# Two gated attention and mixture-of-experts layers on one core: one store of the second layer's output rows, the attentions' first loads a stage ahead, other counts of filling transposes

## The chip, the cores and the metric

The kernel runs on 1 core of one Trainium2 chip. The metric is the device time of one execution in microseconds (us), lower is better. Before the change it is 845.72 us (median of 3 runs, 845.16 to 845.79). A difference of about 0.2% (1.7 us) is what a measurement of this kernel can tell from no change.

## The reference, cut to what matters

Two layers, each a gated cross-attention and then a gated mixture of experts, over x of 8 batches x 256 tokens x 256 features (2048 tokens), all in float32:

```python
x = x + tanh(g_xattn[0]) * attention0(layernorm(x), ctx)        # 16 heads of 16, keys and values from ctx
x = x + tanh(g_ffn[0])   * moe0(layernorm(x))                   # 8 experts, top 2, gelu, biases
x = x + tanh(g_xattn[1]) * attention1(layernorm(x), ctx)
x = x + tanh(g_ffn[1])   * moe1(layernorm(x))                   # 7 experts and a no-op one, top 2, capacity 256

# moe1: weights = softmax(router logits); keep the top 2; each expert takes its first 256 tokens
combined = zeros.at[used_idx].add(relu(inputs @ inter) @ out * in_w)
combined = combined + x_flat * (noop_w * noop_mask)             # the no-op expert's rows
```

So the second layer's result for each token is a sum of three things: x after the attention, its normalised row times its no-op weight, and up to two rows from experts.

## The kernel before, in words

The program is five stages one after the other, each closed by a barrier of all engines that also clears its semaphores (line 77): a small one for constants, then for each layer an attention stage and a stage of routing and experts. Within a stage each engine (SP issues plain DMAs; POOL, ACT, DVE and PE compute; POOL also issues indirect DMAs) runs a list written out by hand, in order, with semaphore waits. An instruction that waits holds up all behind it on its engine.

**Constants** (`constants_phase`): SP loads the gates; POOL makes the identity matrix and index tables; DVE makes the head masks; ACT takes the tanh.

**Attention** (`attention_phase`), by batches b = 0 to 7 of 256 tokens. At its start SP issues, in this order: x of batch 0, Wq, bq, ctx 0, Wk, bk, x of batch 1, Wv, bv, ctx 1, x 2, bo, Wo, and the rest. DVE takes moments of batch 0, POOL turns them into a scale (`rows_scale`, L299 and L301), DVE normalises (L579), PE transposes (`x_transpose(0)`), ACT writes the high part of the transposed rows (L427) and DVE the low part (`inputs_low`, L651), and PE makes `queries(0)`. Each matrix is kept as a high and a low part: ACT writes the high one (`weight_high`, L462) and waits for the weight's load and its bias's by one semaphore; DVE writes the low one (`weight_low`, L647). ctx is split by POOL (`split_context`, L335 and L337). Where PE would stand still, transposes of the identity keep it busy (`fill_first`, `fill_last`, L98); their counts are written in PE's list. In layer 0 DVE first makes nine small tables for the routing (`route_constants`, L551 to L561). At the end of each batch SP stores the normalised rows xr to `xw` (L269) and x to `x1` in layer 0, to `out` in layer 1 (L271), 256 KB each.

**Routing** (`route_phase`): a chain of small DVE instructions over the logits gives the list of tokens per block of 256 slots (`token_of`). Its tables lie in the memory of the x tile and in a tile `more`. In layer 1 ACT meanwhile multiplies xr by the no-op weights (L1258, 16 instructions).

**Experts** (`expert_phase`), by blocks: 23 in layer 0 (16 of 256 slots, 7 of 128), 7 in layer 1. Per block, two sets of 1 MB of weights are loaded (in layer 0 by POOL's indirect DMA at L1161, in layer 1 by SP at L1538 and L1541), split into high and low parts by ACT (L1616, L1624) and DVE (L1688, L1699), the block's rows are gathered by POOL (`load_x`, L1556), transposed by PE (`turn`, L1786), split by ACT (L1656) and DVE (`inputs_low`, L1757), and multiplied. PE's order is first product of block b, in which the rows of block b+1 are turned after the third of four parts, and then the second product of block b-1. Between the products ACT evacuates (L1632 or L1635) and DVE splits the hidden values (`hidden_parts`, L1711 and L1713). DVE's order in a block puts `inputs_low(b + 1)` behind three of the four `hidden_parts`. POOL adds the weighted results to DRAM rows by indirect accumulating DMAs (`add_to_tokens`, L1581).

In layer 1, POOL's list runs: rows of blocks 0, 1 and 2; then four DMAs that add the scaled xr to `out` in DRAM (L1596, 512 KB each, `accum_op`); then for each block b the rows of block b+3 and the additions of block b. The first additions wait for those four DMAs. SP's list in layer 1's experts runs: weights of block 1's first half done, then `load_weights(b)` for b = 0, 1, ...: first set of block b+2, second set of block b+1, each behind the split that frees its buffer.

Of the kernel before, what the change touches and what calls it, by code (L numbers as in the profile page):

```python
# [9 lines left out]
ALU = mybir.AluOpType  # L10
# [90 lines left out]
def attention_phase(nc, layer, shared, dram):  # L101
# [4 lines left out]
    with ExitStack() as ctx:  # L106
# [15 lines left out]
        w_raw = {n: sb(f"{n}_raw", [P, KC, D]) for n in ("wq", "wk", "wv", "wo")}  # L122
# [89 lines left out]
        def _(sp):  # L212
            ctx_src = dram["ctx_t"].rearrange("(k p) n -> p k n", p=P)
            w3 = {n: dram[n].rearrange("(k p) n -> p k n", p=P) for n in ("wq", "wk", "wv", "wo")}
# [19 lines left out]
            def load_weight(n, done):  # L234
                sp.dma_start(w_raw[n][:, :, :], w3[n]).then_inc(done, 16)
# [12 lines left out]
            sp.dma_start(bo[:, :], dram["bo"]).then_inc(wo_ld, 16)  # L248
            load_weight("wo", wo_ld)
# [14 lines left out]
            x_dst = dram["out" if layer else "x1"][0:N, :].rearrange("(t p) d -> p t d", p=P)  # L264
# [27 lines left out]
            sp.wait_ge(x_stored, 16 * B)  # L292

        @block.gpsimd
        def _(pool):
# [34 lines left out]
            def split_context(b):  # L330
                pool.wait_ge(ctx_ld[b % CB], 16 * (b // CB + 1))
# [3 lines left out]
                pool.tensor_copy(hi[:, :, :], ctx_raw[b % CB][:, :, :]).then_inc(ctx_hi, 1)  # L335
                pool.wait_ge(ctx_hi, b + 1)
                pool.tensor_tensor(lo[:, :, :], ctx_raw[b % CB][:, :, :], hi[:, :, :].bitcast(F32), ALU.subtract).then_inc(ctx_split, 1)  # L337
# [56 lines left out]
        def _(act):  # L394
# [12 lines left out]
            def queries(b):  # L407
                wait(act, st_ps, CH * (b - 2))
                if b == 0:
                    act.wait_ge(wq_ld, 32)  # L410
                project(b, q_ps, q_evac, bq, q_s[b % 3][0])

            def keys(b):
                if b == 0:
                    act.wait_ge(wk_ld, 32)
# [42 lines left out]
            loads = {"wq": wq_ld, "wk": wk_ld, "wv": wv_ld, "wo": wo_ld}  # L458

            def weight_high(n):  # L460
                act.wait_ge(loads[n], 32)
                act.activation(w[n][0][:, :, :], w_raw[n][:, :, :], ACT.Copy).then_inc(w_hi[n], 1)  # L462

            def scale_bias():
                act.wait_ge(wo_ld, 32)
# [83 lines left out]
        def _(dve):  # L549
# [14 lines left out]
            def moments(b):  # L564
                if b < XP:
# [16 lines left out]
            def values(b):  # L582
                if b == 0:
                    dve.wait_ge(value_ones_set, 1)
                    dve.wait_ge(wv_ld, 32)
# [74 lines left out]
            if layer == 0:  # L660
                route_constants()
# [7 lines left out]
            moments(2)  # L669
            values(0)  # L670
# [91 lines left out]
        def _(pe):  # L762
# [150 lines left out]
            fill_first(24)  # L913
            x_transpose(0)
            fill_first(12)
            queries(0)
            fill_first(8)
            keys(0)
            fill_first(8)
            values(0)  # L920
            head_scores(0, 0)
            fill_first(4)
            x_transpose(1)
            head_scores(0, 1)
            fill_first(5)
            head_scores(0, 2)
            fill_first(6)
            queries(1)
            head_scores(0, 3)
            fill_first(4)  # L930
            head_scores(0, 4)
            keys(1)
            head_scores(0, 5)
            fill_first(4)
            head_scores(0, 6)
            values(1)
            head_scores(0, 7)
            fill_first(3)
            x_transpose(2)
            fill_first(4)  # L940
            max_transpose(0)
            fill_first(4)
            head_scores(1, 0)
            queries(2)
            head_scores(1, 1)
            scores(0, 0)
            head_scores(1, 2)
            keys(2)
            head_scores(1, 3)
            weigh_values(0, 0)  # L950
# [1001 lines left out]
```

## Time and profile before

| | us |
|---|---|
| median of 3 runs | 845.72 (845.16 to 845.79) |
| profiled execution, its own time | 845.71 |
| its span (first to last instruction) | 844.0 |
| PE busy | 752.9 (89%) |
| DVE busy | 603.9 (72%) |
| ACT busy | 478.4 (57%) |
| POOL busy | 382.4 (45%) |
| DMA moved | 103.45 MB |

The page shows, for each engine, its busy time; then busy tenths in 40 slices of 21.1 us; then DMA queues, the chain of work that ended last, and the costliest groups of instructions. In the slices PE's digit is 9 nearly everywhere; it falls at the start of each layer (slices 1 and 24), in the routing of each layer (slices 11 and 12, 34 and 35), at slice 37 (from 760 us) inside layer 1's experts, and at the end. The stages, by the first instructions behind each barrier: attention 0 from 4.6 us, routing and experts 0 from 214.1, attention 1 from 502.5, routing and experts 1 from 711.7. Lines are those of the kernel before.

### The profile page before, as it was taken

Reading aid. Unit: us, or ns where it says so; the run is one execution under the profiler, and the core shown is the slowest. Engines: PE = TensorE matmul, PEld = TensorE weight load, DVE = VectorE, ACT = ScalarE, POOL = GpSimd, SP = SyncE. Lnnn points to the kernel's source line nnn. Section 1 sums busy time; section 2 is a strip of 40 time slices with the busy share of each in tenths; the row PEclk is TensorE's granted clock in tenths of the full one; section 3 lists DMA queues with packets and bytes.
Section 4 is the critical chain, followed back from the end, with each engine's and each line's share of the span. In section 5 each row is a group of like instructions: output and inputs, shape, how many; then the busy total and the mean of one; then the engine's idle time right before and its main releaser. Section 6 shows DMA issues by size and latency. Waiting matters only on the chain. (4 is left out here: it accounts for less than half of the span.)

```text
span 844.0 us, 17413 instructions
## 1 busy us (share of the span) xinstructions
PE 752.9 (89%) x6872; PEld 636.0 (75%) x6872; DVE 603.9 (72%) x1212; ACT 478.4 (57%) x722; POOL 382.4 (45%) x379
## 2 busy tenths in 40 slices
PE   6999999999469999999999948999999998295995
PEld 5666667667369999999999946666677667295995
DVE  4777777753769998998998916777777734774882
ACT  3376666753056777777676603676667661553640
POOL 6465444112145766666666326645551130252532
PEclk9999999999779999999999979999999999587998
DMA  7001000010377888888888336001000013398642
GB/s 231 15 21 40 27 27 23 9 50 32 98 276 218 243 259 251 256 251 253 254 254 253 74 58 192 14 15 40 27 28 27 28 43 117 97 304 220 165 86 28
DMA packets 47697, 103.45 MB, mean 123 GB/s; under 512 B 9952, under 2 KB 38240, under 8 KB 39936
## 3 DMA queue, kind: packets, MB, share of 16 engines
q0 software_dynamic: 18912, 67.56, 28.0%
q1 hardware_dynamic: 28704, 34.78, 12.3%
q8 instruction: 55, 0.90, 0.4%
q14 instruction: 26, 0.21, 0.1%
HBM read 84.22 MB, written 17.83 MB: 121 GB/s over the span
## 5 line engine op out<-in xcount | busy, mean ns | idle before, releaser
L598 DVE TENSOR_REDUCE mx_a<-ps_max_a 128x2 f32<-128x512 f32 x256 | 164.2, 685 | 35.5 <-PE ps_max_a L844 35.2
L89 PE MATMUL ps_h_e<-xe_t_e,w_e 128*128 128x256 f32 (+1 forms) x480 | 137.9, 287 | 6.0 <-DVE xe_t_e L1757 6.0
L450 ACT ACTIVATE prob_a<-ps_st_a 128x2048 f32<-128x2048 f32 x64 | 120.1, 1876 | 29.1 <-PE ps_st_a L863 28.7
L90 PE MATMUL ps_h_e<-xe_t_e,w_e 128*128 128x256 f32 (+1 forms) x480 | 134.9, 281 | 0.0
L91 PE MATMUL ps_h_e<-xe_t_e,w_e 128*128 128x256 f32 (+1 forms) x480 | 134.9, 281 | 0.0
L89 PE MATMUL ps_y_e<-w_e,h_e 128*128 128x256 f32 x424 | 118.5, 279 | 0.0
L90 PE MATMUL ps_y_e<-w_e,h_e 128*128 128x256 f32 x424 | 118.0, 278 | 0.0
L91 PE MATMUL ps_y_e<-w_e,h_e 128*128 128x256 f32 x424 | 117.9, 278 | 0.0
L89 PEld LDWEIGHTS ps_h_e<-xe_t_e,w_e 128*128 128x128 f32 x480 | 93.0, 194 | 8.2 <-DVE xe_t_e L1757 8.2
L91 PEld LDWEIGHTS ps_h_e<-xe_t_e,w_e 128*128 128x128 f32 x480 | 92.7, 193 | 0.0
L90 PEld LDWEIGHTS ps_h_e<-xe_t_e,w_e 128*128 128x128 f32 x480 | 92.7, 193 | 0.0
L844 PE MATMUL ps_max_a<-k_r_a,q_r_a 32*128 32x512 f32 x256 | 82.8, 513 | 4.0 <-DVE mx_a L598 1.1
L318 POOL TENSOR_SCALAR r_var_eps_a<-r_mean_var_a 128x2 f32<-128x2 f32 x16 | 3.6, 228 | 180.0 <-DVE r_mean_var_a L625 180.0
L1161 POOL DMA_INDIRECT w_raw_w<-L_w,block_row x46 | 48.5, 1055 | 80.6 <-DVE b_e L1704 55.4
L1581 POOL DMA_INDIRECT x<-y_e,token_of x39 | 68.6, 1760 | 30.7 <-ACT y_e L1647 17.4
L1556 POOL DMA_INDIRECT xe_e<-normalised_weighted,token_of x53 | 61.7, 1163 | 45.4 <-DVE token_of L1467 28.0
L89 PEld LDWEIGHTS ps_y_e<-w_e,h_e 128*128 128x128 f32 x424 | 79.9, 188 | 0.0
L91 PEld LDWEIGHTS ps_y_e<-w_e,h_e 128*128 128x128 f32 x424 | 79.9, 188 | 0.0
L90 PEld LDWEIGHTS ps_y_e<-w_e,h_e 128*128 128x128 f32 x424 | 79.8, 188 | 0.0
L1713 DVE TENSOR_TENSOR h_e<-hid_e,h_e 128x512 fp32r<-128x512 f32 (+1 forms) x120 | 76.1, 634 | 4.1
L863 PE MATMUL ps_st_a<-q_s_a,k_s_a 32*128 32x256 f32 x1024 | 78.0, 395 | 0.3
L1635 ACT ACTIVATE hid_e<-ps_h_e,b_e 128x256 f32<-128x256 f32 (+1 forms) x184 | 71.0, 445 | 8.1 <-PE ps_h_e L91 7.6
(236 smaller groups left out, 1756.0 us busy)
## 6 DMA issues: line engine op xcount, KB each, us to landing
w_raw_w<-L_w SPq DMA_DIRECT2D x14, 1024.0 KB
ctx_raw_a<-ctx_t SPq DMA_DIRECT2D x16, 256.0 KB, 4.2
normalised_weighted<-xr SPq DMA_DIRECT2D x16, 256.0 KB, 2.2
x_sb<-x SPq DMA_DIRECT2D x8, 256.0 KB
x_sb<-x SPq DMA_DIRECT2D x2, 1024.0 KB, 8.6
x<-x_sb SPq DMA_DIRECT2D x8, 256.0 KB, 2.5
out<-x_sb SPq DMA_DIRECT2D x8, 256.0 KB, 2.5
out<-xr POOLq DMA_DIRECT2D x4, 512.0 KB, 21.9
```

The lines of the kernel that those rows point to most:

```text
L89: pe.matmul(out, lhs[0], rhs[0], start=start, stop=False)
L90: pe.matmul(out, lhs[1], rhs[0], start=False, stop=False)
L91: return pe.matmul(out, lhs[0], rhs[1], start=False, stop=stop)
L450: act.activation(prob[n % 2][:, :, :, :], ps_st[:, :, :, :], ACT.Exp, scale=HD ** -0.5).then_inc(prob_ready, 1)
L598: dve.tensor_reduce(mx[:, q, h:h + HG + 1:HG], ps_max[j][:, :, :], AX.X, ALU.max).then_inc(max_done, 1)
L844: pe.matmul(ps_max[j][:, :, :], q_r[b % 2][r:r + 32, c, q * P:(q + 1) * P], k_r[b % 2][r:r + 32, c, :, :], start=True, stop=True).then_inc ...
L863: ins = pe.matmul(ps_st[:, g, kt, :], k_s[b % 3][c % 2][rows, c // 2, kt * P:(kt + 1) * P], q_s[b % 3][c % 2][rows, c // 2, :], start=True ...
L1161: pool.indirect_dma_start(out=buffers[which + "_raw"][b % 2][:, :], out_offset=None, in_=dram[which], in_offset=bass.IndirectOffsetOnAxis( ...
L1556: pool.indirect_dma_start(out=xe[b % 2][:, q, :], out_offset=None, in_=dram["xw"], in_offset=bass.IndirectOffsetOnAxis(ap=shared["token_of ...
L1581: pool.indirect_dma_start(out=dram["out" if layer else "x1"], out_offset=bass.IndirectOffsetOnAxis(ap=shared["token_of"][:, t:t + 1], axis=0),
L1635: ins = act.activation(hid[jp % 2][:, j, 0:w], ps_h[jp % RB][:, j, 0:w], ACT.Gelu, bias=b1[b % 2][:, 2 * jp + j:2 * jp + j + 1])
L1713: dve.tensor_tensor(h[b % 2][1][:, js, 0:w], hid[jp % 2][:, :, 0:w], h[b % 2][0][:, js, 0:w].bitcast(F32), ALU.subtract).then_inc(h_ready, 1)
```

## The change

Three things, all in one edit.

1. **Layer 1's output.** The attention of layer 1 no longer stores x to `out`. The routing's tables move out of the x tile, into the memory of `more`, `hid`, `y`, `xe` and the second `w2_raw`, so that x stays in its tile. POOL adds the scaled xr to x there, in four `tensor_tensor` instructions of 128x1024, two before the gather of block 2's rows and two behind it; SP stores each quarter once to `out` with a plain DMA, in its list behind `load_weights(0)` and before `load_weights(1)`. POOL's first additions wait for these stores.
2. **First loads.** Wq, Wk, Wv, Wo and ctx 0 and 1 get places in the upper three quarters of the xr tile and semaphores of their own. For layer 0 SP issues x of batch 0, Wq, Wk, ctx 0, Wv and ctx 1 in the constants stage, for layer 1 all six (without x) in the experts stage of layer 0, once four of its blocks are weighed. `route_constants` of layer 0 moves behind `moments(2)` in DVE's list.
3. **Fills.** PE's list is written out once per layer, with other counts of filling transposes at its head: before `x_transpose(0)`, `queries(0)`, `keys(0)` and `x_transpose(1)` they were 24, 12, 8 and 4; they are 12, 6, 4 and 3 in layer 0, and 23, 6, 4 and 3 in layer 1. All other entries are as before.

The diff, cut to its core:

```diff
@@ attention_phase, SP @@
-            load_x(0)
-            load_weight("wq", wq_ld)
+            if layer:
+                load_x(0)
             sp.dma_start(bq[:, :], dram["bq"]).then_inc(wq_ld, 16)
-            load_context(0)
-            load_weight("wk", wk_ld)
             sp.dma_start(bk[:, :], dram["bk"]).then_inc(wk_ld, 16)
             load_x(1)
-            load_weight("wv", wv_ld)
             sp.dma_start(bv[:, :], dram["bv"]).then_inc(wv_ld, 16)
-            load_context(1)
             load_x(2)
             sp.dma_start(bo[:, :], dram["bo"]).then_inc(wo_ld, 16)
-            load_weight("wo", wo_ld)
+            if layer == 0:
+                load_early(sp, 0, shared, dram, ("wo",))
...
                 sp.dma_start(xr_dst[:, tiles, :], xr[:, tiles, :]).then_inc(xr_stored, 16)
-                sp.wait_ge(x_done, b + 1)
-                sp.dma_start(x_dst[:, tiles, :], x[:, tiles, :]).then_inc(x_stored, 16)
+                if layer == 0:
+                    sp.wait_ge(x_done, b + 1)
+                    sp.dma_start(x_dst[:, tiles, :], x[:, tiles, :]).then_inc(x_stored, 16)
@@ ACT: the weights wait for their own loads, the biases' users for the biases @@
             def weight_high(n):
-                act.wait_ge(loads[n], 32)
+                act.wait_ge(first_ld[n], 16)
@@ DVE @@
-            if layer == 0:
-                route_constants()
             moments(0)
...
             moments(2)
+            if layer == 0:
+                route_constants()
@@ PE, layer 0 (layer 1: 23, 6, 4, ..., 3) @@
-            fill_first(24)
+                fill_first(12)
                 x_transpose(0)
-            fill_first(12)
+                fill_first(6)
                 queries(0)
-            fill_first(8)
+                fill_first(4)
                 keys(0)
...
-            fill_first(4)
+                fill_first(3)
                 x_transpose(1)
@@ new @@
+def load_early(sp, layer, shared, dram, names):
+    for n in names:
+        if n[:3] == "ctx":
+            out = shared["first_ctx"][int(n[3:])]
+            src = dram["ctx_t"].rearrange("(k p) n -> p k n", p=P)[:, :, int(n[3:]) * S:(int(n[3:]) + 1) * S]
+        else:
+            out, src = shared["w_raw"][n], dram[f"L{layer}_{n}"].rearrange("(k p) n -> p k n", p=P)
+        sp.dma_start(out[:, :, :], src).then_inc(shared["first_ld"][layer][n], 16)
@@ constants_phase, SP @@
             sp.dma_start(gates[:, :], dram["gates"]).then_inc(g_ld, 16)
+            src = dram["x"].rearrange("(t p) d -> p t d", p=P)
+            sp.dma_start(shared["x"][:, 0:QT, :], src[:, 0:QT, :]).then_inc(shared["first_ld"][0]["x"], 16)
+            load_early(sp, 0, shared, dram, ("wq", "wk", "ctx0", "wv", "ctx1"))
@@ expert_phase, SP @@
+            out_dst = dram["out"][0:N, :].rearrange("(t p) d -> p t d", p=P)
             for b in range(blocks):
                 load_weights(b)
+                if b == 0:
+                    for c in range(TT // CT):
+                        sp.wait_ge(out_summed, c + 1)
+                        tiles = slice(c * CT, c * CT + CT)
+                        sp.dma_start(out_dst[:, tiles, :], shared["x"][:, tiles, :]).then_inc(buffers["out_stored"], 16)
+        if layer == 0:
+            sp.wait_ge(y_ready, 4)
+            load_early(sp, 1, shared, dram, ("wq", "wk", "ctx0", "wv", "ctx1", "wo"))
@@ expert_phase, POOL @@
             elif layer:
-                pool.wait_ge(buffers["out_added"], 16 * (TT // CT))
+                pool.wait_ge(buffers["out_stored"], 16 * (TT // CT))
...
         load_x(1)
         if layer:
-            load_x(2)
-            out_dst = dram["out"][0:N, :].rearrange("(t p) d -> p t d", p=P)
-            for c in range(TT // CT):
+            def add_rows(c):
                 tiles = slice(c * CT, c * CT + CT)
                 pool.wait_ge(buffers["noop_scaled"], c * CT + CT)
-                pool.dma_start(out_dst[:, tiles, :], shared["xr"][:, tiles, :],
-                               accum_op=ALU.add).then_inc(buffers["out_added"], 16)
+                pool.tensor_tensor(shared["x"][:, tiles, :], shared["x"][:, tiles, :], shared["xr"][:, tiles, :],
+                                   ALU.add).then_inc(out_summed, 1)
+            add_rows(0)
+            add_rows(1)
+            load_x(2)
+            add_rows(2)
+            add_rows(3)
             for b in range(blocks):
                 load_x(b + 3)
                 add_to_tokens(b)
```

## Rows read from the trace of the kernel before

**Rows 1.** Chain of waits, experts of layer 1: start us, length us, what.
```profile
748.25 24.28 DMA xe_e<-normalised_weighted,token_of
772.57 1.13 PE ps_x_e L1786 x4
...
786.48 0.48 PE ps_x_e L1786 x4
...
798.03 0.48 PE ps_x_e L1786 x4
```
**Rows 2.** Windows: length, busy of each engine (instructions), PEclk, DMA share, GB/s.
```profile
762.40:772.60 10.20, 0.03 (x1) 0.03 (x1) 4.62 (x7) 0.75 (x2) 0.00 (x0) 0.72 0.90 284
774.00:776.00 2.00, 2.00 (x11) 2.00 (x11) 1.45 (x3) 1.28 (x2) 1.70 (x2) 0.50 0.58 60
```
**Rows 3.** Timeline, POOL: start, us, line, operation, [idle before it and its releaser].
```profile
735.45 0.94 POOL L1556 DMA_INDIRECT xe_e<-normalised_weighted,token_of  x1 [0.30 <-issue]
...
772.72 1.62 POOL L1581 DMA_INDIRECT out<-y_e,token_of  x1 [22.66 <-DMA out<-xr]
```
**Rows 4.** The page, DMA issues: count, KB each, us to landing.
```profile
out<-xr POOLq DMA_DIRECT2D x4, 512.0 KB, 21.9
```
**Rows 5.** By tile xe_e, from 690 us: landing of the gathers.
```profile
DMA to landing us min/median/max: 2.8/4.7/6.8
```
**Rows 6.** Groups by form, POOL: busy us, mean ns.
```profile
L314 POOL TENSOR_TENSOR x_sb<-x_sb,tgbo_a 128x512 f32<-128x512 f32 x16 | 20.4, 1283 | 0.7
```
**Rows 7.** Timelines of POOL and DVE at the start of layer 1.
```profile
508.53 1.80 POOL L337 TENSOR_TENSOR ctx_t_lo_a<-ctx_raw_a,ctx_t_hi_a 128x512 fp32r<-128x512 f32 x1
...
508.52 0.68 DVE L647 TENSOR_TENSOR wq_lo_a<-wq_raw_a,wq_hi_a 128x512 fp32r<-128x512 f32 x1
509.31 1.57 DVE L647 TENSOR_TENSOR wk_lo_a<-wk_raw_a,wk_hi_a 128x512 fp32r<-128x512 f32 x1
```
**Rows 8.** Timelines of DVE and PE, experts of layer 1, blocks 0 to 2.
```profile
737.55 0.17 DVE L1751 COPY slot_weight_e<-xe_e 128x2 f32<-128x2 f32 x1 [3.33 <-ACT xe_t_e L1656]
...
744.68 0.43 DVE L1711 CAST h_e<-hid_e 128x512 fp32r<-128x512 f32 x1 [0.59 <-ACT hid_e L1632]
...
756.82 0.69 DVE L1757 TENSOR_TENSOR xe_t_e<-ps_x_e,xe_t_e 128x512 fp32r<-128x512 f32 x1
...
757.96 0.28 PE L89 MATMUL ps_h_e<-xe_t_e,w_e 128*128 128x256 f32 x1
```
**Rows 9.** Timeline, SP: the issue of block 3's first weights.
```profile
739.14 0.43 SPq L1538 DMA_DIRECT2D w_raw_w<-L_w  x1
```
**Rows 10.** Timelines of SP, DVE and PE at the start of the program.
```profile
0.80 0.39 SPq L1090 DMA_DIRECT2D gates_sb<-gates  x1
...
3.47 0.21 DVE L1105 TENSOR_SCALAR one_row<-in_pair_f 128x1 f32<-128x1 f32 x2
...
4.66 5.00 PE L98 MATMUL ps_st_a<-ident 128*128 128x128 f32 x24 [4.66 <-PEq L77]
5.06 0.46 SPq L235 DMA_DIRECT2D wq_raw_a<-L_wq  x1
...
7.44 0.75 DVE L570 BATCH_NORM_STATS2 stats_a<-x_sb 128x6 f32<-128x256 f32 x2 [0.69 <-DMA x_sb<-x]
...
14.21 0.36 PE L89 MATMUL ps_lin_a<-xn_t_hi_a,wq_hi_a 128*128 128x256 f32 x1 [1.70 <-DVE xn_t_lo_a L651]
```
**Rows 11.** Timelines of DVE and PE at the start of layer 1.
```profile
505.27 0.75 DVE L570 BATCH_NORM_STATS2 stats_a<-x_sb 128x6 f32<-128x256 f32 x2 [13.65 <-DMA x_sb<-x]
...
511.63 0.36 PE L89 MATMUL ps_lin_a<-xn_t_hi_a,wq_hi_a 128*128 128x256 f32 x1 [1.01 <-DVE xn_t_lo_a L651]
```
**Rows 12.** Waits of SP: us in total, times, longest.
```profile
SPq L292 <- DMA out<-x_sb: 2.0, 1, 2.0
```
**Rows 13.** Timelines of POOL and ACT, experts of layer 0: a weight set's issue and first use.
```profile
295.28 0.97 POOL L1161 DMA_INDIRECT w_raw_w<-L_w,block_row  x1 [0.81 <-DVE b_e L1704]
...
310.44 1.07 ACT L1624 ACTIVATE w_e<-w_raw_w 128x1024 fp32r<-128x1024 f32 x1
```

More of the change, by code:

```diff
@@ L120, in halves @@
             return [sb(f"{name}_{part}", shape, F32R) for part in ("hi", "lo")]
-        w_raw = {n: sb(f"{n}_raw", [P, KC, D]) for n in ("wq", "wk", "wv", "wo")}
+        w_raw, first_ctx, first_ld = shared["w_raw"], shared["first_ctx"], shared["first_ld"][layer]
         w = {n: halves(n, [P, KC, D]) for n in ("wq", "wk", "wv", "wo")}
@@ L262, in _ @@
             xr_dst = dram["xw"][0:N, 0:D].rearrange("(t p) d -> p t d", p=P)
-            x_dst = dram["out" if layer else "x1"][0:N, :].rearrange("(t p) d -> p t d", p=P)
+            x_dst = dram["x1"][0:N, :].rearrange("(t p) d -> p t d", p=P)
             def store_router_rows(b):
@@ L564, in moments @@
             def moments(b):
-                if b < XP:
+                if b == 0 and layer == 0:
+                    dve.wait_ge(first_ld["x"], 16)
+                elif b < XP:
                     dve.wait_ge(x_ld[b], 16)
@@ L930, in _ @@
[L930 to L947, printed above, removed]
@@ L993, in _ @@
-            head_scores(B - 2, 0)
-            weigh_values(B - 4, 2)
-            head_scores(B - 2, 1)
-            queries(B - 1)
-            scores(B - 3, 0)
-            head_scores(B - 2, 2)
-            router_turn(3)
-            weigh_values(B - 4, 3)
-            router_logits(3)
-            head_scores(B - 2, 3)
-            turn_heads(B - 4, 1)
-            keys(B - 1)
-            head_scores(B - 2, 4)
-            scores(B - 3, 1)
-            head_scores(B - 2, 5)
-            values(B - 1)
@@ L1169, in route_phase, with sb @@
     tg = shared["tanh_g"][:, 2 + layer:3 + layer]
-    spare = [shared["x"][:, :, :].rearrange("p a b -> p (a b)"), tiles["more"][:, :]]
-    room = [TT * D, MORE]
-    taken = [0, 0]
-    def sb(name, shape, dt=F32, home=0):
+    spare = [tiles["more"][:, :]] + [tile[:, :, :].rearrange("p a b -> p (a b)") for tile in tiles["later"]]
+    spare.append(buffers["w2_raw"][1][:, 0:FC * D])
+    room = [MORE] + [math.prod(tile.shape[1:]) for tile in tiles["later"]] + [FC * D]
+    taken = [0] * len(spare)
+    def sb(name, shape, dt=F32):
         n = math.prod(shape[1:])
         words = n if dt in (F32, I32) else n // 2
+        home = [i for i in range(len(spare)) if taken[i] + words <= room[i]][0]
         at = taken[home]
         taken[home] += words
-        assert taken[home] <= room[home], name
         ap = spare[home][:, at:at + words]
@@ L1526, in expert_phase @@
     listed, comb_stored = sem("listed"), sem("comb_stored")
-    tiles = {"more": sb("more", [P, MORE]), "ps_h": ps_h, "ps_y": ps_y, "listed": listed, "comb_stored": comb_stored}
+    tiles = {"more": sb("more", [P, MORE]), "later": hid + y + xe, "ps_h": ps_h, "ps_y": ps_y, "listed": listed, "comb_stored": comb_stored}
     def sync_part(sp):
@@ L1869, in sb @@
             return ctx.enter_context(nc.sbuf_tensor(name, shape, dt))
+        sem = semaphores(nc, ctx)
         shared = {
@@ L1898, in program @@
         }
+        shared["w_raw"] = {n: shared["xr"][:, TT // 2 + KC * i:TT // 2 + KC * (i + 1), :] for i, n in enumerate(("wq", "wk", "wv", "wo"))}
+        shared["first_ctx"] = [shared["xr"][:, TT // 4 + KC * i:TT // 4 + KC * (i + 1), :] for i in range(2)]
+        first = ("wq", "wk", "ctx0", "wv", "ctx1", "wo")
+        shared["first_ld"] = [{n: sem(f"{n}_first{layer}") for n in first} for layer in range(2)]
+        shared["first_ld"][0]["x"] = sem("x_first0")
         constants_phase(nc, shared, dram)
```

478 lines of the change are left out of this document (338 added, 140 removed).

## The prediction, made before the changed kernel ran

> **What bounds the kernel now.** The page first: PE is busy 752.9 us, 89% of the span (the table above), so a change that leaves PE's work alone can win only where PE stands still or runs at its lower clock. The slices of the page say where that is: the start of each layer, the routings, and one hole inside layer 1's experts. The chain of waits then names the hole. From 748.25 us it runs for 24.28 us through the landing of one gather of rows, and from 772.57 through PE's turn of them [rows 1]. Later turns are 11.55 us apart (798.03 - 786.48), the length of a block that waits for nothing; the turn at 786.48 comes 13.91 us behind the late one [rows 1]. The windows show PE idle from 762.4 to 772.6 with the 16 DMA engines 90% busy, and then at a granted clock of 0.50, the 1.2 GHz level [rows 2].
>
> That late gather is block 3's. On POOL's queue it stands behind the four accumulating DMAs to `out`, which landed a median of 21.9 us after their issue [rows 4]; other gathers took 2.8 to 6.8 us, 4.7 in the median [rows 5]. The first additions of expert results waited 22.66 us for the same four DMAs [rows 3], but nothing of PE's hangs on those.
>
> **The hole in layer 1's experts: 12.8 us to win.** PE began block 2 at 757.96 [rows 8] and turns block 3's rows after 36 of a block's 96 matmuls, 4.2 to 4.3 us on at 11.55 / 96 each: due at 762.2, it came at 772.57: 10.4 us. The following block took 13.91 - 11.55 = 2.4 us more, at the lower clock for its first part. Sum 12.8 us. In the new kernel block 3's gather is issued behind four POOL additions and no accumulating DMA. POOL is free from 735.45 + 0.94 = 736.4 [rows 3]. One addition of 128x512 takes 1.283 us [rows 6], one of 128x1024 is estimated at 2.5. Two of them end at 741.5, the gather of block 2 at about 744 (needed 11.55 us before 762.2, at 750.6; with 4.7 us of landing it comes at 748, with 6.8 at the very edge), the other two at 749 to 750, and block 3's gather is issued by 752 and there by 757 to 759, for 762.2. So the wait goes, unless a queue is fuller than I think. ACT's scaling of xr, which the additions wait for, is over by then.
>
> **What takes its place: POOL against DVE, 4.1 us back.** At the start of layer 1, POOL's L337 was begun at 508.53 and took 1.80 us, not its usual 1.27, while DVE's `wq_lo` ran to 509.20; then DVE's `wk_lo`, begun at 509.31, took 1.57 us instead of 0.68, and ended 0.55 us behind POOL's instruction [rows 7]. Read together, the two engines took turns, each waiting for the whole of the other's. These DVE instructions have two inputs in SBUF. Now the additions 3 and 4 fall at 744 to 749, where DVE has its densest work of just that kind (hidden values, weight parts). If they shut each other out, DVE loses 2 x 2.5 = 5.0 us, less its pause of 0.59 at 744.68 [rows 8]: 4.4. Its slack is small: the low part of block 2's rows was ready at 756.82 + 0.69 = 757.51, and PE began block 2 at 757.96 [rows 8], 0.4 us of slack, since that instruction stands behind six of the hidden ones and four weight parts. So PE waits 4.4 - 0.4 = 4.0, and about 0.1 for a copy of slot weights that the first addition may hold; 4.1. Bounds: 0, if the pair is not exclusive or DVE always goes first, and 5.5 (4.4 - 0.4, and 1.5 if the copy ahead of `inputs_low(0)`, at 737.55 [rows 8], waits for the end of the first addition at 738.95). I take 4.1, from the row that shows the taking of turns. Later blocks catch up: DVE has 10.3 us of work in 11.55. Net 12.8 - 4.1 = 8.7.
>
> The Trainium skill has a rule that speaks against this change here: "GPSIMD Engine Reference", section "Specifications", says that GpSimd's SBUF interfaces are shared with VectorE, in contention where a DVE instruction has two SBUF inputs or a 2-port mode. The trace agrees [rows 7]. By the page the DMA issue moved to arithmetic costs DVE something; without it the net would read 12.8.
>
> **SP's list in that stage.** Behind `load_weights(0)` SP now waits for the four additions, issues four stores (0.33 to 0.47 us each) and only then block 3's first weights, which were issued at 739.14 [rows 9] and will be at about 751. Also behind: block 2's second set (before 749.20, now 751.5). They are first used at 755.2 and 761.5. At 5.9 us from issue to use for such a set when it was waited for (ACT's first weights of layer 0), the first comes at 757: ACT splits it 2 us later than before, which its own pauses cover. I cost this at nothing; without cover it is 2 us. The four plain stores are issued between 739 and 751 and are there by 756; POOL's first additions need them at 760.5. The 2 MB go out once instead of twice (stored, then read and rewritten), so the engines are emptier.
>
> **The attention of layer 1** gives up eight stores on SP, which is idle there; only the last counts: SP's last wait was 2.0 us for it [rows 12], issued 0.4 us behind the store of xr, which now is the last. 0.2 us, between 0 and 0.5.
>
> **Start of layer 0: 2.2 us.** SP now issues six more loads before the first barrier: each takes up to 0.46 us and some 0.05 to the next [rows 10], so from 1.2 it ends at 4.2, where DVE ended at 3.7 [rows 10] and PE began 0.97 later. The barrier moves to 5.15. But x of batch 0 has landed, and DVE's nine tables are out of the way: moments begin at 5.2 instead of 7.44. From there the queries began 6.77 us on (14.21 - 7.44) in layer 0 [rows 10] and 6.36 us on (511.63 - 505.27) in layer 1 [rows 11], where the weights came no later than needed. 5.2 + 6.36 = 11.56, for 14.21: 2.65 us. From the queries to the first head scores both layers took 7.1 us, and the rest of the attention 191 us in both, so the shift carries through. Against it: PE's fills fell from 24 to 12, so there is a pause of about 1 us before the first transposes; the 24 ran at 0.208 us each (5.00 / 24) [rows 10]. If the higher level comes later, 12 matmuls of queries and as many of keys cost 0.1 us each more. I take 0.45 off: 2.2. Bounds: 4 (moments that no other load delays, weights split early, no taking of turns) and 0 (both products at 1.2 GHz, 2.4 us). The moved tables, about 2 us, fit DVE's idle 5 us before `values(0)`.
>
> **Start of layer 1: 0.4 us.** x of batch 0 still can be loaded only behind the barrier. The 6.36 us stay, because the piece that sets them is `wk_lo` behind POOL's L337 [rows 7], and ctx 0 landing earlier only lets POOL begin 0.2 us sooner, into the same taking of turns. The x load shares the engines with fewer others: 0.4, between -0.4 (POOL gets in between DVE's two `xn` instructions) and 1.2.
>
> **Loads of 1.5 MB in layer 0's experts**, at about 297 us: a second weight set there was issued at 295.28 and first used at 310.44 [rows 13], 15 us for a landing of 5 to 6. Nothing; without cover 3 to 5.
>
> **The sum** against the profiled execution's own 845.71: 8.7 + 0.2 + 2.2 + 0.4 = 11.5, so 834.2. The median of the runs is 845.72, the same.
>
> **The rivals.**
> - *No taking of turns.* All 12.8 come back: 845.7 - 15.6 = 830.1. For it: before, POOL was at its DMA issues in the same stretch and DVE hardly slower. Against it: rows 7. 25%.
> - *The starts give nothing:* the barrier is later and the clock is lower, and in layer 1 POOL gets in first. 845.7 - 8.9 = 836.8. 12%.
> - *Block 3's rows stay late,* as two stores and three weight sets share the engines with their gather: at 15 us of landing instead of 4.7 they come at 767, so that 5 us of waiting and the 2.4 us of lower clock stay, and DVE's loss hides in them: 12.8 - 7.4 = 5.4 won, with 2.8 elsewhere 837.5. For it: 24.28 us in rows 1; against it: the accumulating DMAs are what filled the queue. 7%.
> - *Slower: SP is held by the additions.* If DVE goes first at each turn, additions 3 and 4 finish late, and SP, which waits for them, issues no weights for blocks 2 to 4. With the fourth addition ending at T, block 3's first set is issued at T + 0.4, there 5.9 later and split 4.6 later (its halves at 2 us on ACT, then DVE), needed at 769.8. PE waits T + 10.9 - 769.8, plus 2.4 for the clock. That exceeds all that is won (15.6) from T = 772, 9 us an addition instead of 2.5. Then 846 and more, 848 at T = 774. DVE's pauses before that make it unlikely: 3%.
> - *The change does not do what it says:* the early loads or stores cost what they save somewhere, 844 to 847: 3%.
>
> **How the numbers follow.** The forecast has 50%, its own range 832 to 836.5. The range 829 to 839 takes in the rivals down to 830.1 and up to 837.5, and the bounds of the unknown costs. Faster by over 0.2% (1.7 us, about what a measurement of this kernel can tell from no change): 0.94. Within: 0.02. Slower: 0.04.
>
> **What would show each step.** No DMA_DIRECT2D on POOL; a turn of block 3 with no wait for its gather; four POOL TENSOR_TENSOR of 128x1024 at about 2.5 us each; DVE instructions of hidden and weight parts beside the last two at well over 0.69 and 1.22 us; PE waiting some 4 us in all for `inputs_low` or hidden parts in blocks 1 and 2. Moments at 5.2 and queries at 11.6 in layer 0; moments to queries still near 6.4 in layer 1. It would be wrong if DVE's instructions keep their length beside POOL's (then 830), if PE still waits for a gather, or if PE waits for `w_raw_w` through SP's order.

## The result: 843.26 us, a fifth of what was forecast

| | median of the runs, us | from to (runs) | profiled execution, own time | its span |
|---|---|---|---|---|
| before | 845.51 | 844.7 to 848.66 (20) | 845.71 | 844.0 |
| changed | 843.26 | 839.73 to 846.31 (20) | 844.3 | 842.6 |

The ratio is 0.9969, 95% interval 0.9957 to 0.9982: faster by 0.3%, 2.3 us, where 11.5 were forecast. The changed kernel's runs spread over 6.6 us, those of before over 4.

**Where the time went.** Three marks cut the two spans; all are instructions of the two traces.

| us | before | changed | won | forecast |
|---|---|---|---|---|
| start to layer 0's first head scores | 21.32 | 22.73 | -1.41 | 2.2 |
| first head scores to layer 1's first moments | 483.95 | 483.94 | 0.0 | 0 |
| layer 1: first moments to first head scores | 13.47 | 17.53 | -4.06 | 0.4 |
| first head scores to last router logits | 189.96 | 189.81 | 0.15 | 0 |
| last logits to the end (attention's tail, routing, experts) | 135.3 | 128.59 | 6.7 | 8.9 |

The sum is 1.4, the difference of the spans. Against the forecast 3.6 us are missing in layer 0's start, 4.5 in layer 1's and 2.2 in the last part.

**The hole is gone.** The waits of PE behind 715 us in the changed kernel (what PE waited for: us in total, times, longest):

```profile
PE ps_x_e L1979 <- DMA xe_e<-normalised_weighted,token_of: 6.7, 1, 6.7
PE ps_h_e L1457 <- DVE w_raw_w L1632: 6.5, 2, 5.9
PE ps_h_e L89 <- DVE xe_t_e L1950: 6.2, 3, 4.8
```

Only the first rows of the stage are still waited for; the late gather of [rows 1] is gone, and the turns of blocks 3 to 5 are 11.55 us apart. The second row is the routing, whose tables now lie in the memory of the second `w2_raw`; before, PE waited 6.0 us there too. The third row has grown: PE waits for DVE's low part of the rows, 6.2 us in all, where before it waited 1.5 us once. The chain of waits says why (start us, length us, what):

```profile
740.90 1.15 PE ps_x_e L1979 x4
742.05 0.02 issue
742.07 0.61 ACT xe_t_e L1849
742.68 0.02 issue
742.70 3.52 DVE slot_weight_e L1944
746.23 0.60 DVE xe_t_e L1950
```

A copy of 128x2 elements that took 0.17 us [rows 8] takes 3.52. POOL's timeline of the same stretch, then DVE's:

```profile
740.58 0.95 POOL L1745 DMA_INDIRECT xe_e<-normalised_weighted,token_of  x1 [0.30 <-issue]
741.55 4.64 POOL L1783 TENSOR_TENSOR x_sb<-x_sb,xr 128x1024 f32<-128x1024 f32 x2
747.09 0.97 POOL L1745 DMA_INDIRECT xe_e<-normalised_weighted,token_of  x1 [0.90 <-DVE xe_t_e L1950]
748.37 0.94 POOL L1745 DMA_INDIRECT xe_e<-normalised_weighted,token_of  x1 [0.30 <-issue]
749.33 4.72 POOL L1783 TENSOR_TENSOR x_sb<-x_sb,xr 128x1024 f32<-128x1024 f32 x2
```
```profile
742.70 3.52 DVE L1944 COPY slot_weight_e<-xe_e 128x2 f32<-128x2 f32 x1 [3.40 <-ACT xe_t_e L1849]
746.14 0.68 DVE L1950 TENSOR_TENSOR xe_t_e<-ps_x_e,xe_t_e 128x512 fp32r<-128x512 f32 x1
750.47 3.88 DVE L1904 CAST h_e<-hid_e 128x512 fp32r<-128x512 f32 x1 [3.65 <-ACT hid_e L1825]
754.39 0.69 DVE L1906 TENSOR_TENSOR h_e<-hid_e,h_e 128x512 fp32r<-128x512 f32 x1
```

The additions take 2.3 to 2.4 us each, near the 2.5 forecast. But DVE's copy ends at 746.22, behind both additions (746.19), and its cast at 754.35, behind both of the second pair (754.05). DVE did not get in between two additions: it waited for the whole pair. Nor does a wait in POOL's list let it in as such: each addition has one ahead of it, for ACT's scaling, but it was long met, and the second addition began without a gap.

**The same at both starts.** Layer 0, timelines of DVE, POOL and PE:

```profile
5.11 0.75 DVE L570 BATCH_NORM_STATS2 stats_a<-x_sb 128x6 f32<-128x256 f32 x2 [1.42 <-PEq L77]
7.42 3.54 DVE L579 TENSOR_SCALAR xn_a<-x_sb,mean_var_a,rstd_a 128x256 f32<-128x256 f32 x2 [1.27 <-POOL rstd_a L296]
```
```profile
7.47 0.61 POOL L335 CAST ctx_t_hi_a<-xr 128x512 fp32r<-128x512 f32 x1
8.16 1.26 POOL L337 TENSOR_TENSOR ctx_t_lo_a<-xr,ctx_t_hi_a 128x512 fp32r<-128x512 f32 x1
9.36 1.45 POOL L352 MEMSET v_a<- 128x512 f32 x3
10.76 0.66 POOL L335 CAST ctx_t_hi_a<-xr 128x512 fp32r<-128x512 f32 x1
```
```profile
11.01 1.12 PE L766 MATMUL ps_lin_a<-ident,xn_a 128*128 128x128 f32 x4 [3.11 <-DVE xn_a L579]
11.92 1.49 PE L98 MATMUL ps_st_a<-ident 128*128 128x128 f32 x6
14.40 0.55 PE L89 MATMUL ps_lin_a<-xn_t_hi_a,wq_hi_a 128*128 128x256 f32 x1 [1.00 <-DVE xn_t_lo_a L651]
14.75 0.41 PE L90 MATMUL ps_lin_a<-xn_t_hi_a,wq_lo_a 128*128 128x256 f32 x1
```

Moments begin at 5.11, as forecast. The two xn instructions together took 0.73 us in layer 0 before, 0.41 each with some overlap. Here POOL's L335 began 0.05 us behind the start of the first, which took 0.81 and ended 0.14 behind L335, in the gap of 0.08 us that POOL leaves before L337. The second took 2.81: it ended 0.14 behind the last of the three memsets, so it was kept out through L337 and all of them. The next L335 did not hold it, although it began without a gap (10.76, while the last memset lasted to 10.81). Why DVE got in there is not explained; what stood before it is a memset, which reads nothing. PE, its fills done, stood still for 3.11 us and came back at 0.22 us a matmul (14.75 to 14.97), where run e7 below has 0.12 to 0.13. Layer 1 shows the same: moments at 506.67, xn 3.42 us, an idle 3.29 us of PE, queries at 515.85, 9.18 us behind the moments instead of 6.36 [rows 11], and a window inside them at a granted clock of 0.50, the 1.2 GHz level, with the same 0.21 to 0.22 us a matmul (the column of layer 0's start reads 1.00 all through, so there the pitch has to tell):

```profile
517.00:519.00 2.00, 2.00 (x12) 2.00 (x11) 1.13 (x6) 0.15 (x1) 0.00 (x0) 0.50 0.02 7
```

### The profile page after: what moved, and what is told of

Its sections match the earlier page's. It is cut to its first block and busy times, and to the rows that moved or that the text cites. A ratio compares the mean times of both kernels' runs of the same rounds, so it can differ in the third digit from the quotient of the medians.

```text
span 842.6 us, 17351 instructions
## 1 busy us (share of the span) xinstructions
PE 752.0 (89%) x6837; PEld 634.0 (75%) x6837; DVE 616.1 (73%) x1212; ACT 477.6 (57%) x722; POOL 385.9 (46%) x379
## 5 line engine op out<-in xcount | busy, mean ns | idle before, releaser
L1881 DVE TENSOR_TENSOR w_e<-w_raw_w,w_e 128x1024 fp32r<-128x1024 f32 x60 | 72.6, 1218 | 1.2 <-ACT w_e L1809 1.2
```

Of the source, the lines that this page charges most:

```text
L1881: ins = dve.tensor_tensor(w1[b % 2][1][:, k, :, :], w1_raw[b % 2][:, k * F:(k + 1) * F].rearrange("p (j f) -> p j f", j=FC), w1[b % 2][0][ ...
```

## The experiments

Theory HOLD: a DVE instruction that needs what POOL's run holds waits until POOL pauses for a semaphore, however many instructions the run has. Rival TURNS, the forecast's: the two alternate instruction by instruction. In all of them "before" ran on the same chip; the ratio and its interval are against it. Times are medians of the runs; xn is the length of the pair in layers 0 and 1, the marks are those above (first head scores of layer 0, last logits of layer 0, moments to first scores in layer 1, last logits to the end).

| | us (from to, runs) | ratio, 95% | xn | scores 0 | logits 0 | start 1 | last part |
|---|---|---|---|---|---|---|---|
| before | 845.5 | | 0.73, 1.03 | 21.32 | 211.12 | 13.47 | 135.3 |
| changed | 843.26 (839.73 to 846.31, 20) | 0.9969, 0.9957 to 0.9982 | 3.54, 3.42 | 22.73 | 212.55 | 17.53 | 128.6 |
| e1_store_once | 838.33 (837.85 to 839.57, 4) | 0.9902, 0.9882 to 0.9923 | 0.74, 0.74 | 21.46 | 211.25 | 13.59 | 127.7 |
| e2_early_only | 850.36 (846.8 to 852.52, 12) | 1.0042, 1.0027 to 1.0057 | 3.44, 3.41 | 22.81 | 212.61 | 17.73 | 135.5 |
| e3_gap | 841.94 (838.98 to 845.38, 9) | 0.9948, 0.9927 to 0.9969 | 1.03, 3.41 | 18.59 | 208.57 | 18.04 | 128.3 |
| e4_dve_adds | 838.96 (835.54 to 845.46, 6) | 0.9916, 0.9883 to 0.9949 | 3.41, 3.44 | 23.45 | 213.24 | 17.89 | 123.4 |
| e5_start_gap | 839.39 (838.44 to 841.5, 6) | 0.992, 0.9907 to 0.9934 | 2.14, 2.06 | 20.29 | 210.16 | 15.38 | 129.3 |
| e6_start_wait | 839.13 (838.66 to 839.36, 6) | 0.9918, 0.9905 to 0.9931 | 0.74, 0.73 | 17.92 | 210.62 | 12.36 | 128.4 |
| e7_fills | 842.81 (841.73 to 843.99, 6) | 0.9963, 0.9949 to 0.9978 | 3.56, 3.41 | 21.55 | 211.74 | 16.85 | 128.3 |
| e8_both | 831.84 (831.2 to 833.99, 5) | 0.9834, 0.9818 to 0.9849 | 0.73, 0.74 | 17.43 | 211.45 | 12.34 | 123.1 |
| e9_both_fills | 832.15 (831.85 to 832.58, 5) | 0.984, 0.9823 to 0.9857 | 0.73, 0.73 | 19.41 | 209.44 | 12.34 | 122.7 |
| e10_once_dve | 833.85 (833.26 to 834.57, 4) | 0.9862, 0.9841 to 0.9882 | 0.73, 0.73 | 21.04 | 210.82 | 13.84 | 122.2 |
| e11_ones_first | 830.94 (830.16 to 831.54, 5) | 0.9825, 0.9808 to 0.9842 | 0.73, 0.73 | 18.74 | 208.72 | 12.27 | 122.8 |
| e12_late_ctx | 842.75 (839.86 to 851.08, 12) | 0.9975, 0.9955 to 0.9995 | 0.73, 3.41 | 17.47 | 211.14 | 17.58 | 128.2 |

**The two halves of the change.** e1_store_once is the kernel before with part 1 alone; e2_early_only is the changed kernel with part 1 taken back, so parts 2 and 3 alone.

> The kernel before with part 1 alone (x summed by POOL, stored once); starts of both attentions as before. In the changed kernel's trace the attention of layer 1 ends 5.3 us later than before, and the experts stage is 6.5 us shorter. Theory HOLD (a DVE instruction that needs the shared access waits through a whole run of POOL instructions that has no semaphore wait inside; the starts lose by that, and the additions cost DVE 3.4 + 3.5 us): about 845.5 - 6.7 = 838.8, DVE's slot-weight copy and its first cast of hidden values 3 to 4 us long each. Rival TURNS (the engines take turns instruction by instruction, and the rest of the loss is DMA or clock): copy and cast not over 2.6 us, time 836 to 838. If the two parts hinder each other (xr used by both): clearly above 840.

> The changed kernel with part 1 undone (x stored by the attention, xr added by POOL's accumulating DMAs): parts 2 and 3 alone. HOLD: both starts lose, 1.4 us in layer 0 and 4.0 us in layer 1, in the profile each by DVE's second normalising instruction held for about 2.8 us behind POOL's split, memsets and next split, and by queries at the 1.2 GHz level: about 850 to 851. Rival: the starts gain as I predicted and the changed kernel lost its time elsewhere: 842 to 843.

Both came as HOLD expected. Part 1 alone is 1.0% faster than before, parts 2 and 3 alone are 0.4% slower. In e2 both xn pairs are held (3.44, 3.41). In e1 both POOL pairs hold DVE, 3.62 and 3.90 us, with ordinary starts, so the two losses are separate.

**Additions with a pause.** e3_gap makes POOL wait for its own last addition:

```diff
                 pool.wait_ge(buffers["noop_scaled"], c * CT + CT)
+                wait(pool, out_summed, c)
                 pool.tensor_tensor(
```

> The changed kernel with one wait more: each of POOL's additions waits for the semaphore of the one before it, which puts a pause of some 0.08 us between them. HOLD: DVE's slot-weight copy gets in behind the first addition (about 1.3 us instead of 3.5), the first cast behind the third (about 2.3 instead of 3.9): 2 us or so less, 841. TURNS, or a hold by anything but POOL's run of instructions: no change, 843.3.

DVE's timeline in e3:

```profile
739.80 1.27 DVE L1945 COPY slot_weight_e<-xe_e 128x2 f32<-128x2 f32 x1 [3.35 <-ACT xe_t_e L1850]
740.98 0.68 DVE L1951 TENSOR_TENSOR xe_t_e<-ps_x_e,xe_t_e 128x512 fp32r<-128x512 f32 x1
745.31 3.33 DVE L1905 CAST h_e<-hid_e 128x512 fp32r<-128x512 f32 x1 [3.65 <-ACT hid_e L1826]
748.68 2.74 DVE L1907 TENSOR_TENSOR h_e<-hid_e,h_e 128x512 fp32r<-128x512 f32 x1
```
```profile
738.69 4.86 POOL L1784 TENSOR_TENSOR x_sb<-x_sb,xr 128x1024 f32<-128x1024 f32 x2
...
745.91 4.95 POOL L1784 TENSOR_TENSOR x_sb<-x_sb,xr 128x1024 f32<-128x1024 f32 x2
```

The copy now ends at 741.07, in the pause behind the first addition, and the cast at 748.64, between the third and the fourth; the next instruction is then held through the fourth. Both pauses are 0.15 us long. So the pause is what lets DVE in: this is what TURNS had assumed for every pair of instructions. The cast took 3.33 us, not the 2.3 expected. It was begun 0.60 us ahead of the third addition and did not go through before it; POOL was at the issue of a gather then (744.96 to 745.91), with the addition 0.01 us behind it, so the issue may count as part of the run, but no run tests that. The pauses let DVE in but gave no time back here: the last part is 128.3 us against 128.6, and what the median gained (841.94 against 843.26) lies within the spread of both and goes with a start of layer 0 that was not held (below).

**Additions on DVE.** e4_dve_adds (changed kernel) and e10_once_dve (the e1 kernel) put the four additions into DVE's list:

```diff
-                pool.tensor_tensor(shared["x"][:, tiles, :], ...
+            dve.tensor_tensor(shared["x"][:, tiles, :], ...
...
+                if layer:
+                    add_rows(0)
+                    add_rows(1)
                 inputs_low(0)
+                if layer:
+                    add_rows(2)
+                    add_rows(3)
```

> The changed kernel with the four additions on DVE instead of POOL, two before and two behind the low part of block 0's rows, where DVE stands still; SP's stores as they are. HOLD and TURNS alike say that without additions on POOL no DVE instruction is stretched in blocks 0 to 2: four times 1.22 us on DVE in its pauses, the experts stage shorter by about 6 us than the changed kernel's: 837 to 838. If the loss in this stage is SP's order or the DMA queues instead: 841 to 843.

> The kernel before with part 1 alone (output stored once), its four additions on DVE. HOLD: the 4.3 that DVE and PE lost come back, 838.3 - 4.3 = 834.0; no DVE instruction of blocks 0 and 1 is stretched. If POOL's additions cost nothing themselves (the loss was at the starts): 838.

DVE does each in 1.22 us, about half of POOL's 2.36:

```profile
734.89 2.35 DVE L1765 TENSOR_TENSOR x_sb<-x_sb,xr 128x1024 f32<-128x1024 f32 x2
738.34 0.17 DVE L1753 COPY slot_weight_e<-xe_e 128x2 f32<-128x2 f32 x1 [1.09 <-ACT xe_t_e L1658]
...
742.75 0.43 DVE L1713 CAST h_e<-hid_e 128x512 fp32r<-128x512 f32 x1 [1.39 <-ACT hid_e L1634]
```

This is e10. No instruction is stretched, and the last part falls by 5.2 us (changed to e4) and 5.5 (e1 to e10): the price of the hold, forecast at 4.1. The medians fall by 4.3 (changed to e4, whose six runs lie 9.9 us apart) and 4.5. Against before, e10's last part is 13.1 us shorter: that is the hole, forecast at 12.8 and 0.2 for the tail.

**A pause, or a wait, at the starts.** e5_start_gap puts a pause of POOL ahead of the memsets, e6_start_wait makes POOL wait for xn:

```diff
             def value_ones():
+                pool.wait_ge(ctx_split, 1)                 # e5
...
             rows_scale(0)
+            pool.wait_ge(normalised_first, QT)             # e6
             split_context(0)
```

> The changed kernel, with a wait of POOL for its own last piece of ctx 0 ahead of the memsets of both attentions' starts. Theory HOLD (a DVE instruction waits through a whole run of POOL instructions that follow each other without a pause, and gets in at a pause for a semaphore): the second xn instruction, which took 2.81 us beside L337 and the memsets, ends behind L337, in about 1.3 us, in both layers; queries 1.5 us earlier, time about 840.5. Theory TURNS (POOL and DVE alternate instruction by instruction): there is nothing to let in, xn stays at 2.8, 843.3.

> The changed kernel, in which POOL begins ctx 0's split only when DVE's two xn instructions of batch 0 are done, in both layers. HOLD: xn takes 0.37 us twice, queries begin near 11.5 us in layer 0 (14.4 in the changed kernel) and 6.4 us behind the moments in layer 1 (9.2 there); about 5 us less in all, 838.3. If the late transposes are not xn's doing but the clock's or the fills', queries move by under 1 us and the time stays at 842 to 843.

POOL's timeline in e5, then DVE's:

```profile
8.15 1.26 POOL L337 TENSOR_TENSOR ctx_t_lo_a<-xr,ctx_t_hi_a 128x512 fp32r<-128x512 f32 x1
9.47 1.48 POOL L353 MEMSET v_a<- 128x512 f32 x3
```
```profile
7.42 2.14 DVE L580 TENSOR_SCALAR xn_a<-x_sb,mean_var_a,rstd_a 128x256 f32<-128x256 f32 x2 [1.27 <-POOL rstd_a L296]
9.48 0.68 DVE L648 TENSOR_TENSOR wq_lo_a<-xr,wq_hi_a 128x512 fp32r<-128x512 f32 x1
```

L337 and the memsets overlapped by 0.06 us in the changed kernel (8.16 + 1.26 against 9.36); now they are 0.06 apart, and xn ends at 9.56 instead of 10.96. A pause of 0.06 us is worth 1.4 us of DVE's time. With the wait in e6 xn takes 0.74 in all, and the runs, 6.6 us apart in the changed kernel, lie within 0.7. e6 gained 4.1 us of the 5 expected; in both layers PE now waits for batch 1's rows (1.4 and 0.8 us), and part of the gain is lost again, as in e8 below.

**The clock.** e7_fills takes part 3 back, with 24, 12, 8 and 4 fills.

> The changed kernel with the old counts of filling transposes (24, 12, 8, 4) in both layers. If the fewer fills cost the starts their clock: queries and keys at the 2.4 GHz pitch, 1.2 to 2.5 us less per layer, 839 to 841, with xn as long as in the changed kernel. If only the hold of xn counts: within 1 us of the changed kernel's 843.3.

xn is as long as before, but layer 0's queries run at 0.12 us a matmul, and from queries to head scores it takes 7.11 us again instead of 8.33; in layer 1 7.69 instead of 8.35 (the first queries still run at 0.21 us a matmul there, behind PE's wait). So the fills' part in the marks is 1.2 and 0.7 us, the hold's 2.4 to 2.8 each. In the medians only 0.45 us show, within both spreads.

**Both holds away.** e8_both is e4 and e6 in one, e9_both_fills has the old fills too.

> The changed kernel with both holds taken away: the four additions on DVE (two ahead of block 0's inputs_low, two behind it), and POOL's split of ctx 0 behind the two xn instructions. HOLD: both gains are whole and add up: 4.3 (additions) and 5 (starts) below the changed kernel's 843.3, about 834.2, the time that was predicted for the change. If the two do not add up (a later stage takes the starts' gain back), 837 to 839.

> The changed kernel with both holds taken away (additions on DVE, POOL's split of ctx 0 behind xn) and the old counts of filling transposes (24, 12, 8, 4). If the clock that falls behind the first head scores (0.50 from 22 to 28 us in that kernel's trace) comes from the short fills: it stays at 1.00 and some 2 us come back, 829.5 to 830.5. If the fills only hold up the transposes (24 of them last to 9.2 us, the rows are there at 8.2): 831.8 to 833.

831.84: a larger gain than was forecast for the change, and faster than e1. By the last parts and starts the two gains add (e6's span 837.5 less 5.3 is 832.2, e8's is 831.9). But of the 3.9 us that layer 0 had won by its first scores (17.43 against 21.32) none is left at its last logits. PE's waits from 17 to 60 us, and the windows (length, busy of PE, PEld, DVE, ACT, POOL, PEclk, DMA share, GB/s), both e8:

```profile
PE ps_lin_a L767 <- POOL xn_a L303: 1.8, 1, 1.8
```
```profile
16.00:20.00 4.00, 2.41 (x17) 1.79 (x17) 3.22 (x9) 1.07 (x2) 3.81 (x4) 1.00 0.69 215
20.00:24.00 4.00, 3.70 (x16) 2.30 (x17) 2.66 (x5) 0.60 (x1) 0.16 (x1) 0.73 0.02 6
24.00:28.00 4.00, 4.00 (x19) 3.49 (x17) 0.42 (x1) 0.46 (x2) 0.00 (x0) 0.50 0.00 0
```

Batch 1's rows come from POOL, which is busy from 8.2 to 20.2 us with no gap over 0.15; PE waits, and then runs at the 1.2 GHz level. In e9, where the longer fills delay the first batch by 2.0 us, that wait and the fall of the clock are both gone, and the last logits are 2.0 earlier; the total is the same within its interval, so the 2 us that were expected back do not show in the medians.

**The memsets first.** e11_ones_first is e8 with the memsets where POOL had nothing to do:

```diff
+            value_ones()
             rows_scale(0)
             pool.wait_ge(normalised_first, QT)
             split_context(0)
-            value_ones()
```

> The changed kernel with both holds taken away, and POOL's three memsets at the start of each attention put ahead of the first moments' scale, where POOL is idle (1.2 us in layer 0, 3.8 in layer 1). In the kernel without this move PE waited 1.8 us for batch 1's rows, which POOL normalises behind the memsets, and ran at the 1.2 GHz level from 22 to 28 us. Expected: batch 1's rows 1.4 us earlier, the wait under 0.6, the clock whole, 3 us less in layer 0 and 0.5 to 1.5 in layer 1: about 828.5. If the clock falls all the same: 831.

PE's waits from 17 to 60 us and the windows in e11:

```profile
PE ps_lin_a L767 <- POOL xn_a L303: 0.2, 1, 0.2
```
```profile
22.00:26.00 4.00, 4.00 (x27) 3.06 (x26) 2.55 (x5) 0.84 (x2) 0.00 (x0) 1.00 0.00 2
```

The wait and the low clock behind it are gone as expected, and layer 0's last logits come 2.4 us ahead of before's. But not for the reason expected: POOL began batch 1's rows at 17.41 us instead of 17.72, 0.3 earlier and not 1.4, since it now waited 0.4 us for the queries and some of its casts took longer. Most of the wait went because PE came later: its first queries ran at 0.21 us a matmul, and the first head scores stand at 18.74 instead of 17.43. The traces agree on this. Where the first head scores of layer 0 came at 17.4 to 17.9 us (e6, e8, e12), PE waited 1.4 to 1.8 us for batch 1's rows, and the way to the last logits took 192.7 to 194.0 us; where they came at 18.59 or later (all others), it took 189.8 to 190.2. The median fell by 0.9 us to 830.94, not by 3.3: e8's profiled run was one of its slowest (833.99). This is the fastest kernel of the study, 1.75% under before; against e8 the intervals overlap.

**What set the stall off.** e12_late_ctx is the changed kernel with ctx 0 alone loaded behind the attention's first barrier again:

```diff
             sp.dma_start(bk[:, :], dram["bk"]).then_inc(wk_ld, 16)
+            load_early(sp, layer, shared, dram, ("ctx0",))
             load_x(1)
```

> The changed kernel in which ctx 0 alone is loaded behind the attention's first barrier again (behind the biases of Wq and Wk), all else as changed. If the early landing of ctx 0 is what sets the stall off (POOL finds it there and starts its run right behind DVE's first xn instruction): in layer 0 ctx 0 now lands near 8.3 us, behind both xn (8.15); xn takes 0.7 to 1.0, queries begin near 11.5 to 12 (14.4 in the changed kernel). In layer 1 x is 1.2 us longer under way before the moments, so ctx 0 lands close to the end of rstd and either may win. 843.3 - 2.7 = 840.6 if layer 1 stays held, 837.5 if it does not. If DVE's second xn waits for something else than POOL's run: no change, 843.3.

POOL's and DVE's timelines in e12, layer 0:

```profile
8.95 0.61 POOL L336 CAST ctx_t_hi_a<-xr 128x512 fp32r<-128x512 f32 x1 [2.02 <-DMA xr<-ctx_t]
```
```profile
6.97 0.73 DVE L580 TENSOR_SCALAR xn_a<-x_sb,mean_var_a,rstd_a 128x256 f32<-128x256 f32 x2 [1.27 <-POOL rstd_a L297]
```

With ctx 0 late, POOL begins behind xn, which takes 0.73 us, and queries begin at 10.38, 4.0 us earlier than in the changed kernel (0.45 of it because the moments begin at 4.66, one load fewer standing ahead of the barrier). In layer 1 ctx 0 had landed before POOL had the scale, and xn is held (3.41). Here too layer 0's gain is gone by the last logits (211.14; wait for batch 1's rows 1.5 us), and the median is that of the changed kernel within the spread, not the 840.6 expected. So the early landing of ctx 0 is shown as the trigger of the stall in layer 0, and taking the trigger away in this manner gained nothing that the spread would let one see.

## Why the prediction was wrong, point by point

- **The hole, 12.8 us: right.** 13.1 with the tail, shown by e10 against before. Block 3's gather was not waited for, and no wait on `w_raw_w` came through SP's order: block 3's first weights were issued at 754.50.
- **POOL against DVE, 4.1 us back: right in place and sign, wrong in mechanism, small.** It measured 5.2 (e4), 5.5 (e10), at the upper bound of 5.5. Of the two pauses the forecast named, the copy of slot weights, which it charged with 0.1, was held 3.5 us, because the hold lasts for the pair and not to the end of the first addition (738.95 in its words). The rest of the 2.2 missing in the last part, about 1 us, is the changed kernel's longer last part against e1's (128.6 against 127.7). Nearly all of that lies behind PE's last instruction, where POOL's last additions go out (10.7 us against 9.9); it is not explained.
- **Start of layer 0, 2.2 us: the failing step, with the next.** The sentence that failed is "5.2 + 6.36 = 11.56": it took the way from moments to queries as fixed. It was 9.29. The forecast had asked what the early loads would save, not what else they would release: ctx 0 in place released POOL's run of split, subtraction and memsets at 7.47, 0.05 us behind the start of the first xn. Before, ctx 0 came too late for that. The clock was charged 0.45 and cost 1.2.
- **Start of layer 1, 0.4 us: the same failure.** The case was seen, "POOL gets in between DVE's two xn instructions", and priced at -0.4, one 0.6 us instruction of POOL's. Priced by the run behind it (from L337 to the last memset, 2.65 us in layer 1) it is -2.4; measured were 9.18 us instead of 6.36 to the queries, and 8.35 instead of 7.11 from there to the head scores, at the low clock. It stood in a rival with 12% ("POOL gets in first") and only as a start that gives nothing.
- **Why rows 7 misled.** There DVE's `wk_lo` took 1.57 us beside POOL's L337 and ended 0.55 us behind it [rows 7], with POOL's three memsets already running: they began at 510.28 and took their ordinary 1.44 us. So DVE did get in behind one instruction, and I read it as the rule. But the one behind was a memset, which reads nothing, and `wk_lo` is a TENSOR_TENSOR. xn, a TENSOR_SCALAR, is held by the same memsets, and a TENSOR_TENSOR is held by an addition, which reads (L1907 in e3, 2.74 us instead of 0.69). What follows in POOL's run, and of what kind, had to be asked; one pair cannot show it. The same trace had the hold in xn itself:

```profile
507.57 1.03 DVE L579 TENSOR_SCALAR xn_a<-x_sb,mean_var_a,rstd_a 128x256 f32<-128x256 f32 x2 [1.26 <-POOL rstd_a L301]
```
```profile
507.76 0.69 POOL L335 CAST ctx_t_hi_a<-ctx_raw_a 128x512 fp32r<-128x512 f32 x1 [0.23 <-DMA ctx_raw_a<-ctx_t]
```

  The pair took 1.03 us instead of 0.73, and ended at 508.60, 0.15 behind POOL's L335; it got in at the gap before L337.
- **The rest:** tail 0.2 against 0.2 (routing began 1.65 us behind the last logits' end instead of 1.85), SP's list 0, the loads in layer 0's experts 0 (483.94 against 483.95 us between the marks), all as forecast.
- **The spread.** In the profiles of the changed kernel, e2, e3, e4 and e7, whose attention code is the same but for e7's fills, xn was held at nine starts of ten. At the tenth (e3, layer 0) POOL had to wait for ctx 0's landing and began 0.09 us later, 0.14 behind the start of the first xn. POOL's timeline, then DVE's:

```profile
7.56 0.74 POOL L335 CAST ctx_t_hi_a<-xr 128x512 fp32r<-128x512 f32 x1 [0.17 <-DMA xr<-ctx_t]
8.38 1.82 POOL L337 TENSOR_TENSOR ctx_t_lo_a<-xr,ctx_t_hi_a 128x512 fp32r<-128x512 f32 x1
```
```profile
7.42 1.03 DVE L579 TENSOR_SCALAR xn_a<-x_sb,mean_var_a,rstd_a 128x256 f32<-128x256 f32 x2 [1.27 <-POOL rstd_a L296]
```

  Now the first xn went through in its ordinary 0.41 us. The second took 0.70: L335 alone held it, and it got in at the gap of 0.08 us before L337, where in the changed kernel the first had got in and the second had been left to the whole run. Head scores came at 18.59, 2.7 us ahead of before's, as the forecast had added up before it took 0.45 off for the clock. So the forecast's start exists, in the runs in which a race of a tenth of a microsecond goes that way. That this makes the spread of 6.6 us is a guess: e6's six runs, where there is no race, lie 0.7 us apart, but e7's six, with the race, lie 2.3 apart, and the runs of before, whose starts are not held, 4.0. Single runs leave no trace to show it.

The Trainium skill, "SBUF — State Buffer", section "SBUF: two separate sides", says that of a DVE and a GpSimd instruction the one that starts first has the shared ports for its whole length and the other is fully blocked, and that a DVE instruction is concerned in a 2-port mode or with two SBUF inputs, the latter only against a GpSimd instruction that reads SBUF. The rows agree: `wk_lo` passed the memsets, and xn did not. They go further in one thing: the one that waits stays out through the other's following instructions too, as long as these come without a gap. Gaps of 0.06 us (e5), 0.08 (before L337) and 0.15 (e3) let it in. The one instruction without a gap before it that did not hold xn is the second L335, behind the memsets; what lets DVE in there is open.

## What to carry to other kernels

Before work is put on POOL beside a busy DVE, or a load is made earlier that POOL waits for, list the run of POOL instructions that then follows without a gap (a wait that is met long before makes none), and charge a DVE instruction that falls into it with the whole run (memsets too, if it is a TENSOR_SCALAR, COPY or CAST from SBUF), not with one instruction; a small wait inside the run, or POOL waiting for DVE's critical pair first, took 4 us off here. When the first batch is made earlier, look at who makes the second batch's rows, and when: here they came at 19.8 to 20.6 us, and a first batch ready by 17.4 won nothing over one ready by 18.7, since PE's wait and the lower clock behind it gave all of the gain back.

## What the runs showed of the hardware that was not expected

- A DVE copy of 128x2 elements, 0.163 us in the median, took 3.52 us beside two POOL additions; a cast with one input in SBUF (0.42) took 3.88; TENSOR_SCALAR of 128x256 took 2.81 beside a subtraction and three memsets, which read nothing.
- POOL is held too: in e6 its L335, begun at 8.22, takes 1.60 us, 0.61 in the changed kernel; it ends 0.47 us behind the second of two DVE weight parts (8.07 to 9.35) that followed each other.
- DVE adds 128x1024 floats in 1.22 us, POOL in 2.36.
